# A graph network kernel: parts of a unit between logits, ScalarE's first sums in the last attended tile, and four incidence tiles in period 6

## The reference

```python
for n in range(2):                        # top-p attention, TOP_P = 0.9
    q = X @ W1.T @ W2.T;  k = X @ W3.T
    probs = softmax(q @ k.T)              # 2048 x 2048
    keep = largest probs of each row, until their sum reaches 0.9
    A = probs * keep / sum(probs * keep)
    Xf = R @ Xf                           # R = adj + I, rows divided by their sum
    Xa = A @ Xa
    Z = Z + Xf @ U1[n].T + Xa @ U2[n].T
h = X + Z
layer2 = (h - mean) / sqrt(var + eps) * ln_g + ln_b
# third layer, first product: m = incidence.T @ relu(layernorm(x))
```

## Time and profile before

| | us |
|---|---|
| median of 3 runs (lowest, highest) | 1072.84 (1069.78, 1074.75) |
| profiled execution | 1073.61 |
| its span, first to last instruction | 1071.8 |
| TensorE busy | 838.4 (78% of the span) |
| VectorE busy | 779.4 (73%) |
| ScalarE busy | 509.2 (48%) |
| GpSimd busy | 70.5 (7%) |

### The profile page before, as it was taken

One profiled execution on the slowest core, in us unless ns is written; L12 is line 12 of the kernel. 1 busy time (PEld: TensorE's weight loads), 2 busy tenths in 40 slices (PEclk: granted clock), 3 DMA queues, 4 the chain that ended last, 5 costly groups with the idle time before them and its releaser, 6 DMA issues.

```text
span 1071.8 us, 12286 instructions
## 1 busy us (share of the span) xinstructions
PE 838.4 (78%) x3886; PEld 563.7 (53%) x3886; DVE 779.4 (73%) x2363; ACT 509.2 (48%) x979; POOL 70.5 (7%) x68
## 2 busy tenths in 40 slices
PE   4879958887887843839778978868289899996795
PEld 4844325555655633737356557547258475553342
DVE  5978679888998998961797889789799502326715
ACT  4877235357367376314452664764765332023212
POOL 0020110000000000000000000010000200002201
PEclk9999987888988985969799789979689999998798
DMA  9949203334004000000044220220152546500001
GB/s 335 354 173 430 104 29 129 130 106 158 1 1 158 1 1 1 1 2 1 1 157 149 87 79 1 94 119 1 49 209 78 230 161 245 226 1 0 1 0 39
DMA packets 20221, 108.25 MB, mean 101 GB/s; under 512 B 1824, under 2 KB 8752, under 8 KB 9776
## 3 DMA queue, kind: packets, MB, share of 16 engines
q1 hardware_dynamic: 18752, 106.77, 26.7%
q10 hardware_dynamic: 1392, 0.61, 0.2%
HBM read 88.23 MB, written 19.14 MB: 100 GB/s over the span
## 4 chain that ended last, share of the span: by engine, by line
PE 47%; DVE 29%; ACT 11%; issue 9%; POOL 2%; DMA 1%; DVEq 1%; POOLq 0%; SPq 0%; ACTq 0%
DVE AT L1525 9%; PE PS L808 9%; PE PS L743 7%; PE PS L676 5%; PE PS L880 5%; PE PS L546 4%; DVE mxv L1664 4%; DVE nd L1528 3%; PE PS L1063 3%; PE PS L1039 3%; DVE AT L2111 2%; PE PS L1069 2%; ACT BC L1252 2%; ACT AT L1252 2%; ACT AT L1085 1%
## 5 line engine op out<-in xcount | busy, mean ns | idle before, releaser
L1085 ACT ACTIVATE AT<-PS 128x512 f32<-128x512 f32 (+2 forms) x240 | 118.2, 562 | 127.1 <-PE PS L546 107.8
L743 PE MATMUL PS<-K,ST 128*128 128x512 f32 x224 | 129.4, 731 | 15.7 <-ACT EA L1220 8.1
L546 PE MATMUL PS<-ident,AT 128*128 128x128 f32 x544 | 84.1, 289 | 42.5 <-DVE AT L1525 18.0
L1525 DVE SCALAR_TENSOR_TENSOR AT<-EA,se 128x2048 uint8<-128x2048 f32 (+1 forms) x46 | 107.6, 2345 | 1.6 <-DVE se L1518 0.3
L1525 DVE SCALAR_TENSOR_TENSOR AT<-AT 128x2048 uint8<-128x2048 f32 (+2 forms) x48 | 96.1, 2002 | 1.8 <-PE PS L546 0.8
L1664 DVE TENSOR_REDUCE mxv<-PS 128x1 f32<-128x2048 f32 x32 | 73.3, 2289 | 30.4 <-PE PS L743 24.7
L546 PEld LDWEIGHTS PS<-ident,AT 128*128 128x128 f32 x544 | 67.5, 150 | 50.9 <-DVE AT L1525 18.9
L743 PEld LDWEIGHTS PS<-K,ST 128*128 128x128 f32 x224 | 50.6, 238 | 78.1 <-issue 78.0
L2111 DVE MAX8 AT<-AT 128x8 f32<-128x256 f32 x256 | 87.6, 411 | 0.7
L808 PE MATMUL PS<-hr,AT 128*128 128x128 f32 x512 | 69.2, 284 | 8.5 <-ACT AT L1085 7.7
L808 PE MATMUL PS<-AT 128*128 128x128 f32 x512 | 67.4, 279 | 10.2 <-ACT AT L1085 9.7
(11 more groups left out here) (297 smaller groups left out, 1471.1 us busy)
## 6 DMA issues: line engine op xcount, KB each, us to landing
AT<-keep_at SPq DMA_DIRECT2D x32, 1024.0 KB, 5.1
EA<-in_adj SPq DMA_DIRECT2D x20, 1024.0 KB, 6.8
keep_at<-AT SPq DMA_DIRECT2D x8, 2048.0 KB, 24.9
AT<-keep_at SPq DMA_DIRECT2D x8, 2048.0 KB, 12.2
AT<-in_adj SPq DMA_DIRECT2D x12, 1024.0 KB, 5.7
EA<-keep_degrees SPq DMA_DIRECT2D x1, 1024.0 KB, 6.4
keep_x<-K SPq DMA_DIRECT2D x4, 256.0 KB, 8.6
out<-EA SPq DMA_DIRECT2D x4, 256.0 KB, 2.3
```

The source lines that it names most:

```text
L546: return pe.transpose(dst, src, ident[0:p, 0:p])
L743: mm = pe.matmul(bank(half(gi, k) + n), ST[1][:, k * P:(k + 1) * P], wide_keys[:, n * BK:(n + 1) * BK], start=True, stop=True)
L1085: return act.activation(dst, src, ACT.Copy)
L1525: return dve.scalar_tensor_tensor(out=o, in0=x0, scalar=s, in1=x1, op0=op0, op1=op1, **k)
```

## The change

- Periods 0 and 4, TensorE: the sums of a unit can be issued in two halves (`unit_part`). The unit behind logits 1 gives its rows only behind logits 2; the third unit has half of its sums behind logits 2 and the other half and its rows behind logits 3; the fourth follows whole. ScalarE's calls for the units follow this order, with the guess between the third and the fourth.
- Last attended tile of periods 1, 2, 5 and 6, ScalarE: the guess goes ahead of `result_out`. Behind the fourth copy and behind the scaled copy stand the first two of the twelve sums, or, in period 6, the second norm and second scaling of block 0. In periods 1 and 5 a third sum stands between the two copies of the query.
- First attended tile of these periods: the exponential of tile 1 goes behind the fourth copy in place of the third.
- `third_sum` of these periods: the row maximum goes behind the second pass in place of the first.
- VectorE, wherever a next block exists: `doubtful_with_sums` in place of `doubtful`, `last_tile`, `surplus_below` and `last_surplus`: the same operations, mixed, with fewer full waits.
- Step 1: the first norm of block 1 goes to period 6 between the sums, its scaling behind the first pair of the second threshold; its turned rows are summed one tile earlier in the attention of period 7. Four incidence tiles in place of three stand in period 6, and one less behind the attention of block 6.

The diff, without its context lines:

```diff
@@ -596,23 +596,22 @@
...
-            def unit_sums(u):
-                p, c = u // UNITS, u % UNITS
+            def unit_freed(u):
...
+            def unit_part(u, h):
+                p, c = u // UNITS, u % UNITS
...
-                for j in range(NT):
-                    if j % HALF == 0:
-                        pe.wait_ge(slab_in[j // HALF], 16 * (u + 1))
+                pe.wait_ge(slab_in[h], 16 * (u + 1))
+                for j in range(h * HALF, (h + 1) * HALF):
...
-                    if j == HALF - 1:
-                        mm.then_inc(un_half, 1)
@@ -745,12 +744,18 @@
...
-            def unit(step, g, u, early=False):
+            def unit_begun(step, g, u, early=False):
...
-                unit_sums(u)
+                unit_freed(u)
+                unit_part(u, 0)
+            def unit(step, g, u, early=False):
+                unit_begun(step, g, u, early)
+                unit_part(u, 1)
@@ -812,18 +817,18 @@
...
-                if normed is not None and k - normed in (1, 2):
-                    rows_turned(normed, k - normed - 1)
+                if normed is not None and k in (1, 2):
+                    rows_turned(normed, k - 1)
...
-                if normed is not None and k - normed in (1, 2):
-                    pe.wait_ge(ln_ts, 2 * normed + k - normed)
-                if normed is not None and k - normed in (2, 3):
+                if normed is not None and k in (1, 2):
+                    pe.wait_ge(ln_ts, 2 * normed + k)
+                if normed is not None and k in (2, 3):
...
-                    rows_summed(normed, k - normed - 2)
+                    rows_summed(normed, k - 2)
@@ -833,9 +838,6 @@
...
-                    if normed == 1:
-                        pe.wait_ge(exT_ok, G * gi + k + 1)
-                        rows_summed(normed, 1)
@@ -846,7 +848,7 @@
...
-                    pe.wait_ge(z_ok, NT + G * (b + 1) + b + h)
+                    pe.wait_ge(z_ok, NT + G * (b + 1) + h)
@@ -933,10 +935,20 @@
...
+                            at = units_by(NB * step) + k
...
-                            if k < UNITS_IN[NB * step]:
-                                unit(step, 0, units_by(NB * step) + k, True)
+                            if k == 2:
+                                unit_rows(at - 1)
+                            if k == 3:
+                                unit_part(at - 1, 1)
+                                unit_rows(at - 1)
+                            if k == 1 or k == 2:
+                                unit_begun(step, 0, at, True)
+                            if k == 1:
+                                unit_part(at, 1)
+                            if k == 0 or k == 3:
+                                unit(step, 0, at, True)
@@ -946,7 +958,7 @@
...
-                        for t in range(3):
+                        for t in range(4):
@@ -962,7 +974,6 @@
...
-            multiplied(3)
@@ -1170,11 +1181,13 @@
...
-            def queries(step, g):
+            def queries(step, g, between=None):
...
+                if between:
+                    between()
@@ -1239,21 +1252,23 @@
...
+                for k in tiles:
+                    for f in range(2):
+                        one_below(step, g, m, k, f)
+            def one_below(step, g, m, k, f):
...
-                n = sums_by(gi, m)
...
-                n += 2 * tiles[0] if g > 0 else 0
-                for k in tiles:
-                    for f, func in enumerate((ACT.Relu, ACT.Sign)):
-                        if n > 1:
-                            act.wait_ge(sum_ok, n - 1)
-                        act.activation(act_junk[f], E[:, k, :], func, scale=-1.0, bias=th[:, k:k + 1],
-                                       accum_out=below[:, f, k:k + 1]).then_inc(sum_ok, 1)
-                        n += 1
-            def attend(step, g, k, between=None, normed=None, inside=None):
+                n = sums_by(gi, m) + f + (2 * k if g > 0 else 0)
+                if n > 1:
+                    act.wait_ge(sum_ok, n - 1)
+                act.activation(act_junk[f], E[:, k, :], ACT.Relu if f == 0 else ACT.Sign, scale=-1.0,
+                               bias=th[:, k:k + 1], accum_out=below[:, f, k:k + 1]).then_inc(sum_ok, 1)
+            def attend(step, g, k, between=None, normed=None, inside=None, copied=None, scaled=None):
@@ -1261,8 +1276,8 @@
...
-                    if normed is not None and k - normed in (0, 1):
-                        turned_out(normed, k - normed)
+                    if normed is not None and k < 2:
+                        turned_out(normed, k)
@@ -1270,8 +1285,8 @@
...
-                    if normed is not None and k - normed in (1, 2):
-                        summed_out(normed, k - normed - 1)
+                    if normed is not None and k in (1, 2):
+                        summed_out(normed, k - 1)
@@ -1280,17 +1295,21 @@
...
+                    if b == 1 and between:
+                        between()
...
-                    if b == 1 and between:
-                        between()
-                    if b == 2 and inside:
+                    if b == 3 and inside:
...
+                if copied:
+                    copied()
...
+                if scaled:
+                    scaled()
@@ -1386,38 +1405,52 @@
...
+                    def first_of_tail(f):
+                        if normed is None:
+                            one_below(step, g + 1, 0, 0, f)
+                        elif f == 0:
+                            second_norm(0)
+                        else:
+                            second_scaled(0)
...
-                    elif normed == 1:
-                        first_norm(1)
...
-                            attend(step, g - 1, k, (lambda: guess(step, g + 1)) if more and k == G - 1 else None, normed,
-                                   inside=(lambda: exponential(step, g + 1, 1)) if more and k == 0 else None)
-                            if normed == 1 and k == 0:
-                                first_scaled(1)
+                            ends = more and k == G - 1
+                            attend(step, g - 1, k, (lambda: guess(step, g + 1)) if ends else None, normed,
+                                   inside=(lambda: exponential(step, g + 1, 1)) if more and k == 0 else None,
+                                   copied=(lambda: first_of_tail(0)) if ends else None,
+                                   scaled=(lambda: first_of_tail(1)) if ends else None)
...
-                        if g == 0:
+                        if g == 0 and k != 2:
...
+                                unit_next()
...
-                        queries(step, g + 2)
+                        queries(step, g + 2, (lambda: one_below(step, g + 1, 0, 1, 0)) if g > 0 else None)
...
-                        sums_below(step, g + 1, 0, (0, 1, 2))
+                        if normed == 0 or g == 0:
+                            sums_below(step, g + 1, 0, (0, 1, 2))
+                        else:
+                            if g == NB - 2:
+                                one_below(step, g + 1, 0, 1, 0)
+                            one_below(step, g + 1, 0, 1, 1)
+                            sums_below(step, g + 1, 0, (2,))
...
-                        if step == 1 and g == 1:
-                            first_norm(0)
+                        if step == 1 and g > 0:
+                            first_norm(g - 1)
+                        sums_below(step, g + 1, 1, (0,))
...
-                            second_norm(0)
-                            sums_below(step, g + 1, 1, (0,))
-                            second_scaled(0)
-                        sums_below(step, g + 1, 1, (1,) if normed == 0 else (0, 1))
+                            first_scaled(1)
+                        sums_below(step, g + 1, 1, (1,))
@@ -1928,11 +1961,11 @@
...
-                if gi not in BOTH:
-                    between()
...
+                if gi not in BOTH:
+                    between()
@@ -2070,6 +2103,36 @@
...
+            def doubtful_with_sums(nq, n):
+                mass_above(EA if n % 2 == 0 else EB, n, G - 1)
+                v.wait(1)
+                v.put(tt(s_(3), s_(3), s_(4), ALU.max))
+                v.put(tt(fl[:, TIE:TIE + G], after, s_(0), ALU.is_ge))
+                v.put(tt(s_(5), seen8, s_(0), ALU.is_ge))
+                v.wait(2)
+                v.put(tt(s_(4), after, s_(0), ALU.is_ge))
+                v.wait(1)
+                v.put(tt(s_(3), s_(5), s_(3), ALU.max))
+                dve.wait_ge(sum_ok, sums_by(n, 0) + 2 * (G - 1))
+                v.put(stt(pa, below[:, 1, :], float(N), ALU.add, nq.th, ALU.mult))
+                v.wait(1)
+                v.put(dve.tensor_reduce(fl[:, UNSURE:UNSURE + 1], s_(3), AX.X, ALU.max))
+                v.put(tt(s_(4), s_(4), s_(3), ALU.max))
+                v.put(tt(pb, below[:, 0, :], nq.spare, ALU.add))
+                v.wait(1)
+                v.put(dve.tensor_reduce(fl[:, 0:1], s_(4), AX.X, ALU.max))
+                v.wait(1)
```

(17 more changed lines are left out.)

## The result

The changed kernel takes 1081.38 us, the median of five runs (1076.52 to 1081.88), where the kernel before takes 1072.84 in the same session. The ratio is 1.0075, with a 95% interval of 1.0059 to 1.0092: 8 us slower. The prediction said 1071.2 us, with a range up to 1077.0, and gave "slower" a chance of 0.14.

The account below looks back on a forecast made before the run. A ring of ScalarE's sums, TensorE's banks and VectorE's logits was taken to bound periods 0 to 6, TensorE from about 825 us. The sum -0.6 + 4.7 - 1.05 - 0.75 + 3.0 - 6.9 = -1.6 gave 1071.2 us, range 1061.5 to 1077.

Parts of the forecast that it names:

- Period 6 and the tail: End of the kernel: freed guess wait, earlier turns, early incidence tiles, second norm and block 2's root sooner; 6.9 us gained.
- Period 1: While VectorE refines query block 1's threshold: sum overruns, early guess and moved maximum delay the unit copy; 4.7 us longer.
- period 5: While VectorE refines query block 5's threshold: same overruns, less 0.2 us gained, delay the unit copy; 3.0 us longer.
- The overruns: Last attended tile, periods 1 and 5: three 2.0 us sums overrun gaps by 0.75, 1.6, 0.8; second query copy 3.15 later.
- The guess ahead of the copies: Last attended tile: guess waits some 0.8 us for input and takes 0.6, costing 1.1 in period 1; period 5 keeps 0.2 gain.
- The moved row maximum: Period 1, second tile: row maximum behind another 2.35 us pass; exponential starts at 274.6 for 272.33, costing 0.4 us.
- Periods 0 and 4: Unit parts: logits come sooner but the fourth unit follows late; the ring is only 0.6 and 0.75 us earlier.
- Period 2: A pass fills VectorE's 1.86 us logits wait; the guess leaves 0.35, doubts add 0.7: 1.05 us gained (0 to 2.5).
- Doubts: VectorE's doubts with sums: new order takes 4.0 us for 4.7, gaining 0.7; little where ScalarE's sums come last.
- TensorE falls to 1.2 GHz before the units: Slower rival, chance 0.14: after longer idling half a unit runs at low clock, 3.7 us more in two periods; 1078.6 us.
- The slip is hidden: Faster rival, chance 0.28: the late query misses the unit's copy, periods 1 and 5 gain 0.9 and 2.0 us; 1060.6 us.
- GpSimd is held: Rival, chance 0.06: a root caught by VectorE's pass costs 2.3 us, one by masks 1.5; net +2.2, 1073.4 us.

Follow-up runs that it names:

- e1: Kernel before with the tail (norms in gaps, four incidence tiles) and the moved row maximum and exponential in period 6 alone: 1065.43 us, ratio 0.9936.
- b1: Kernel before with only the part of the last two blocks (second norm in gaps, four incidence tiles in period 6): 1069.63 us, ratio 0.9964.
- e3: d1 with three incidence tiles in period 6 and the fourth behind the loop, as before the change: 1065.63 us, ratio 0.9938.
- c2: b1 plus ScalarE's first sums in gaps of the last attended tile in periods 1, 2 and 5: 1077.61 us, ratio 1.0045.
- d2: b1 plus the guess ahead of the unit's result, nothing else: 1077.16 us, ratio 1.0039.
- c4: Changed kernel with 20 useless matmuls filling TensorE's waits between the last attended tile and first logits of periods 1 and 5: 1080.64 us, ratio 1.0081.
- a3: Changed kernel with the guess back behind the whole of the unit's result: 1077.85 us, ratio 1.0056.
- a1: Changed kernel with ScalarE's first sums back behind the exponentials, none in gaps; period 6's second norm stays in gaps: 1073.30 us, ratio 1.0008.
- c1: Changed kernel with gap sums in period 2 alone, exponential behind the fourth copy everywhere, row maximum by mistake moved in periods 1 and 5 only: 1074.29 us, ratio 1.0019.
- d4: b1 plus the unit parts of periods 0 and 4, nothing else: 1073.02 us, ratio 0.9999.
- d1: Kernel before with the tail, unit parts in period 4 alone, and the moved row maximum and exponential in period 6 alone: 1066.49 us, ratio 0.9941.
- a2: Changed kernel with the next tile's row maximum back behind the first pass and the exponential behind the third copy: 1090.80 us, ratio 1.0164.
- e2: d2 with the guess of periods 2 and 6 back behind the result, so early in periods 1 and 5 alone: 1074.68 us, ratio 1.0016.
- c3: Kernel before with 12 useless matmuls in TensorE's idle stretches between the last attended tile and first logits of periods 1 and 5: 1077.39 us, ratio 1.0051.
- d3: d1 with four single useless matmuls in TensorE's waits in each of periods 1 and 5: 1068.65 us, ratio 0.9966.

## Why the prediction was wrong, step by step

- **Period 6 and the tail, -6.9: right in size (-7.9), in part by luck.** The first turns of period 7 come 7.0 us earlier against the period's first exponential (79.7 us for 86.7), where 5.4 were forecast, and 0.9 more are won behind them, for 1.5. The freed wait for the guess went to TensorE's turns, as written, but left 2.75 us and not 1.2. Low clock at the first turns, the early incidence tiles and the root of block 2 came as written. The forecast gave the moved row maximum no term of its own here, and it carries about half: e1, with the norms in gaps, four tiles and the maximum and exponential moved in period 6 only, is 7.25 us below the kernel before; without these two moves (b1) only 3.1 stay. e1 leaves the guess in its old place and gains as much, with 3.0 us of wait for it. The fourth tile brings no more, as written (e3).
- **Period 1 +4.7 and period 5 +3.0: the failed terms.** They came out +9.6 and +8.5. The mechanism was right as far as it went: overruns late on TensorE, the unit's copy late, ScalarE's wait longer (8 us or more was the mark, 9.07 came). The sizes were not, in three places. By stretches, period 1 lost 3.6 us in its first three tiles (0.4 forecast) and 6.0 in the last tile (4.3 forecast); period 5 lost 8.3 us in the last tile, which is what the sums alone (5.5, c2) and the guess alone (2.9, d2) cost there.
  1. *The overruns, 3.15 us a period.* In period 1 the query's copy is 4.57 us later against the tile's last copy. The two sums ahead of the result's copy make 2.08 of this (2.35 were forecast). The low clock was left out: the projection and the first matmuls of the query, behind the stretches in which TensorE now stands, make 1.60. The last 0.89 stand where the third sum (end 322.70) and the query's slow second matmuls (end 322.82) end together. The query's matmuls take 1.94 and 1.96 us for 1.04 and 1.07; with fillers they were 1.07 (c4). The sums alone cost +6.0 and +5.5 us in the two periods, and 8.0 us over the whole (c2).
  2. *The guess ahead of the copies, 1.1 us in period 1 and 0.9 in period 5, set there against a gain of 1.1.* It costs 7.5 us alone (d2): in period 2 a stop of 1.03 us on TensorE, slower matmuls behind it, and VectorE's pass 2.8 us late. It was priced at its length and its wait for input, with nothing for the slower matmuls. In the changed kernel a3 shows 3.5 us of it, 1.6 and 2.8 us by the last tiles of periods 1 and 5.
  3. *The moved row maximum, 0.4 us in period 1.* The first three tiles are 3.6 us longer than before in the profiled execution, and 0.7 shorter in a1 and a3, which have the same order there. What differs is how far VectorE is when the period begins: in after VectorE's closing reciprocal of period 0 (263.65) starts 0.26 us ahead of ScalarE's first exponential of period 1, in a1 and a3 1.74 us. So in after ScalarE waits 3.03 us for the row maximum and TensorE stands 3.32 us, and the logits of tile 2 then take 6.30 us; in a1 these are 0.64, 0.93 and 3.61.

```profile
277.08 1.97 ACT L1233 ACTIVATE EA<-PS,negmax 128x2048 f32<-128x2048 f32 x1 [3.03 <-DVE negmax L1555]
...
279.72 6.30 PE L742 MATMUL PS<-K,ST 128*128 128x512 f32 x8
```

  The kernels c1 and c4 begin at 0.26 us too and have the long form. Up to there the code of after, a1 and a3 is the same, so none of the edits explains which start comes; that stays open. In period 5 the same start (0.26) costs only the wait: the logits of tile 2 stay fast in after, a1 and a3.
- **Periods 0 and 4, -0.6 and -0.75: wrong in sign for period 0.** The row maximum of tile 3 came at 213.19, 3.6 us earlier than the earlier trace rows has it and 1.8 later than forecast. The fourth unit behind it began at 219.68 and not 217.6, and its last 30 matmuls took 8.02 us where they take 6.64 at full clock, so the query was at 231.18 and not 227. Alone the unit parts cost 3.4 us (d4), an error about as large as the guess's, and in period 4 they win nothing (e1 for d1): the -2.9 us there are given back in period 5.
- **Period 2, -1.05: right as a sum (-1.0) by luck, wrong inside.** The moved maximum wins 3.7 us there beside the sums and the early guess (a2), and the guess holds VectorE's pass 2.8 us (d2).
- **Doubts, -0.7: not tested by itself.** b1 with sums, guess and units alone would be 1069.6 + 8.0 + 7.5 + 3.4 = 1088.5 us; a2, which has all of these and the doubts, takes 1090.8. The 2.3 us left hold the doubts and whatever doesn't add up.
- **The rivals.** "TensorE falls to 1.2 GHz before the units" named the right engine, but put the price on the unit, 3.7 us a period. In period 1 the unit ran at full speed (6.64 us); the low clock was at the query, at the projection ahead of it, and at logits that were slow before the change too. Of the 6.0 us of period 1's last tile, 1.6 to 2.5 lie in the projection and the query. "The slip is hidden" was plainly wrong: the wait for the unit had no slack. "GpSimd is held" has a slip in its sum: +2.2 us on 1072.84 is 1075.0 and not 1073.4, which takes the -1.6 off twice. It came in part: the last step of block 2's root took 1.75 us at 857.77, beside a mask, where the same step of block 0 took 0.20, while block 2's product, this time begun ahead of the mask, took 1.01 us for 3.00.

By the Trainium skill (GPSIMD Engine Reference, Specifications), GpSimd shares SBUF interfaces with VectorE and meets contention from VectorE's instructions that read two SBUF inputs. The trace agrees: 1.55 us more on one operation of 128 x 4 while the mask ran.

## What to carry to other kernels

Work that is longer than the gap it is moved into delays whoever waits behind it. Here its price was more than the overrun, since TensorE, which then stopped, ran its next matmuls slower. Measure a gap at the instruction that will be late, not at the engine that is idle, and ask of every small operation moved ahead of a copy who waits for that copy: four operations of 0.2 us, with up to 0.9 us of waiting for their input, cost 7.5 us here in four places. Where several edits come together, run each alone: of this change the tail and the moves of period 6 were worth 7 us together (e1), and the sums, the guess and the unit parts, each added alone to b1, cost 19. And a mark on an engine that isn't the bound (the exponential of period 4, 3 us early) shows gains that the time doesn't have.

## What was not expected of the hardware

- TensorE's granted clock fell without a long stop. In period 2 of d2 TensorE had stood 2.15 us, run eight products at full speed (1.16 us) and stood 1.03 us; the two matmuls behind took 0.80 us for 0.39, what the lower of the two levels (1.2 and 2.4 GHz) gives. The length of the last stop doesn't decide it: behind a stop of 1.0 to 1.1 us the same two matmuls took 0.49 us in period 5 of d2 and e2 and in period 1 of a1, and behind one of 1.82 us they took 0.49 in all three periods of c2 and 0.80 in period 1 of the changed kernel.
- Filling the waits with matmuls kept the level up in most places: the first logits took 3.70 us in periods 1 and 5 of c3 and c4 and in period 1 of d3, where they took 5.40 to 6.64 without; in period 5 of d3, with four fillers, they stayed at 5.40. A filler of 128 columns by 256 takes 0.52 us.
- The same order of instructions gave two lengths for period 1's first two tiles, from its first exponential to the third: 23.3 us in a1 and a3, 27.6 in after, c1 and c4. The changed kernel's five runs lie at 1081 to 1082 us four times and at 1076.5 once. So one profiled execution bounds a stretch only to some 4 us where such a choice is open.
